# Transposing the quantised rows in fp32, with the rounding constant taken off by ScalarE's copies

## What is computed

```python
x = x + xattn(_layernorm(x), ctx, ctx, Wq, Wk, Wv, Wo, bo, mask)      # 16 heads of 64, causal, softmax
x = x + ffn(_layernorm(x), w_gate, w_up, w_down)

def _act_quant(x):
    scale = 127.0 / jnp.clip(jnp.max(jnp.abs(x), axis=-1, keepdims=True), 1e-05)
    return jnp.clip(jnp.round(x * scale), -128.0, 127.0) / scale
def _bitlinear(x, w):
    return jnp.einsum('bsi,oi->bso', _act_quant(x), _weight_quant(w))
def ffn(x, w_gate, w_up, w_down):
    return _bitlinear(jax.nn.silu(_bitlinear(x, w_gate)) * _bitlinear(x, w_up), w_down)
```

## Time and profile before

| | |
|---|---|
| timed runs | 828.57, 829.24, 829.48 us; median 829.24 |
| the profiled execution | span 827.9 us from its first to its last instruction |
| instructions in it | 17931 |
| mean granted clock of TensorE | 0.991 of full speed |
| HBM read and written | 15.64 MB and 4.19 MB, 24 GB/s over the span |

### The profile page before, as it was taken

How to read it: one execution, slowest core, us unless ns; L and a number is a source line. 1 busy time by engine, 2 the same in 40 slices (tenths; PEclk the granted TensorE clock), 3 DMA queues, 4 the chain that set the end, 5 groups by cost and what they waited for, 6 DMA issues and landing times.

```text
span 827.9 us, 17931 instructions
## 1 busy us (share of the span) xinstructions
PE 781.9 (94%) x5487; PEld 539.4 (65%) x5550; DVE 738.6 (89%) x1909; ACT 679.7 (82%) x1202; POOL 407.3 (49%) x404
## 2 busy tenths in 40 slices
PE   7899999999999999999999999999999999999873
PEld 5657666766766666676666667567666666766552
DVE  6759999999989998999989999899989999988994
ACT  4689888888888888888888898888888888888772
POOL 1235555454544644545455554455554555545551
PEclk9999999999999999999999999999999999999996
DMA  7200010100101010010100101010010100000000
GB/s 214 62 1 1 15 39 15 39 1 15 39 14 38 13 35 4 13 38 13 38 4 21 28 13 38 14 38 0 13 39 13 38 13 13 2 13 14 1 14 13
DMA packets 37108, 20.49 MB, mean 25 GB/s; under 512 B 1460, under 2 KB 36534, under 8 KB 37046
## 3 DMA queue, kind: packets, MB, share of 16 engines
q1 hardware_dynamic: 37046, 19.84, 8.3%
HBM read 15.64 MB, written 4.19 MB: 24 GB/s over the span
## 4 chain that ended last, share of the span: by engine, by line
PE 52%; DVE 31%; issue 11%; ACT 3%; DVEq 1%; POOL 1%; DMA 0%; POOLq 0%; ACTq 0%
PE ps_a L501 9%; PE ps_s L432 7%; DVE row_sum L821 5%; DVE xq_b L839 3%; PE ps_s L403 3%; DVE amax L778 2%; DVE hid L775 2%; PE ps_s L323 2%; PE ps_a L460 2%; PE ps_b L460 2%; PE ps_kv L403 2%; PE ps_s L325 2%; PE ps_kv L323 2%; PE ps_s L404 2%; PE ps_s L324 2%
## 5 line engine op out<-in xcount | busy, mean ns | idle before, releaser
L875 POOL TENSOR_TENSOR prob<-prob,row_max 128x1024 f32<-128x1024 f32 x64 | 122.0, 1906 | 194.1 <-DVE row_max L748 194.1
L521 ACT ACTIVATE vp<-ps_s 64x512 f32<-64x512 f32 x256 | 151.4, 591 | 32.8 <-PE ps_s L405 28.5
L893 POOL TENSOR_TENSOR prob<-prob,row_rec 128x512 f32<-128x512 f32 x128 | 130.9, 1044 | 56.2 <-DVE row_rec L823 56.2
L521 ACT ACTIVATE vp<-ps_kv 64x512 f32<-64x512 f32 x256 | 151.6, 592 | 5.4
L885 POOL TENSOR_TENSOR hid_b<-hid_q,neg_round 128x512 bf16<-128x512 f32 x64 | 66.6, 1041 | 130.1 <-DVE hid_q L792 130.1
L432 PE MATMUL ps_s<-kp,xn_t 128*64 128x512 f32 x512 | 124.0, 605 | 2.9 <-ACT vp L521 1.9
L501 PE MATMUL ps_a<-vp,prob_t 128*64 128x128 f32 x2048 | 125.9, 276 | 0.8 <-DVE x L770 0.6
L501 PEld LDWEIGHTS ps_a<-vp,prob_t 128*64 128x64 f32 x2048 | 110.6, 137 | 24.0 <-issue 16.4
L852 POOL TENSOR_TENSOR rs<-ve,neg_half 128x1 f32<-128x1 f32 x128 | 70.4, 550 | 35.5 <-DVE ve L670 25.4
L745 DVE TENSOR_TENSOR prob<-ps_s,bias_sb 128x1024 f32<-128x1024 f32 x64 | 78.2, 1222 | 10.7 <-PE ps_s L432 9.9
L521 ACT ACTIVATE kp<-ps_s 128x512 f32<-128x512 f32 x130 | 77.8, 598 | 12.0 <-PE ps_s L291 8.2
(11 more groups left out here) (176 smaller groups left out, 1767.6 us busy)
## 6 DMA issues: line engine op xcount, KB each, us to landing
x_in<-in_x SPq DMA_DIRECT2D x16, 256.0 KB, 3.0
ctx_in<-in_ctx SPq DMA_DIRECT2D x16, 256.0 KB, 3.4
x_res<-in_x SPq DMA_DIRECT2D x16, 256.0 KB, 2.8
out<-x SPq DMA_DIRECT2D x15, 256.0 KB, 2.3
kp<-in_L_xattn_Wk SPq DMA_DIRECT2D x1, 512.0 KB, 4.5
kp<-in_L_xattn_Wq SPq DMA_DIRECT2D x1, 512.0 KB, 5.3
kp<-in_L_xattn_Wv SPq DMA_DIRECT2D x1, 512.0 KB, 6.2
kp<-in_L_xattn_Wo SPq DMA_DIRECT2D x1, 512.0 KB, 6.1
```

Of the source, the lines that this page charges most:

```text
L521: copy = lambda dst, src, **kw: nc.scalar.activation(dst, src, ACT.Copy, **kw)
L875: p.tensor_tensor(prob[c % 2][:], prob[c % 2][:], rows(row_max[c % 2]), ALU.subtract).then_inc(shifted, 1)
L893: p.tensor_tensor(prob[c % 2][:, heads, :], prob[c % 2][:, heads, :], rows(row_rec[c % 2])[:, heads, :], ALU.mult).then_inc(normed, 1)
```

## The change

The subtraction of ROUND moves behind the transposes. xq and hid_q stay as fp32 rows that still hold ROUND; PE transposes them with the fp32 identity id_sb that the other transposes use, into fp32 views of the same PSUM banks; ACT's two copies to bf16 get a bias of -ROUND. The tiles xq_b, hid_b, id_bf and neg_round and the instructions that made them are gone. The guard on xqt_ready moves from L839 ahead to the instruction that makes xq, and L792's guard is now ht_ready. A slot has one DVE and one POOL instruction less, and ln2_step counts nine steps for ten.

```diff
-        ps_h = ps_b[:, 0:F // 2].bitcast(BF16)
+        ps_h = ps_b
-        ps_x = ps_u[:, 0:D // 2].bitcast(BF16)
+        ps_x = ps_u[:, 0:P]
...
-        LN1_STEPS, LN2_STEPS, H_STEPS = 3, 10, 7
+        LN1_STEPS, LN2_STEPS, H_STEPS = 3, 9, 7
...
-                    nc.tensor.transpose(ps_x[:, 0:P], xq_b[:], id_bf[:]).then_inc(xqt_ready, 1)
+                    nc.tensor.transpose(ps_x, xq[:], id_sb[:]).then_inc(xqt_ready, 1)
...
-                    pe.wait_ge(hb_ready, s - 2)
+                    pe.wait_ge(hq_ready, s - 2)
                     for k in range(FB):
-                        t = nc.tensor.transpose(ps_h[:, k * P:(k + 1) * P], hid_b[:, k * P:(k + 1) * P], id_bf[:])
+                        t = nc.tensor.transpose(ps_h[:, k * P:(k + 1) * P], hid_q[:, k * P:(k + 1) * P], id_sb[:])
...
-                    copy(xq_t[:], ps_x[:, :]).then_inc(xqt_evac, 1)
+                    copy(xq_t[:], ps_x, bias=-ROUND).then_inc(xqt_evac, 1)
...
-                    copy(flat(hid_t[:, :, :]), ps_h[:, :]).then_inc(ht_evac, 1)
+                    copy(flat(hid_t[:, :, :]), ps_h[:, :], bias=-ROUND).then_inc(ht_evac, 1)
...
-            dve.wait_ge(id_in, 16)
-            v.tensor_copy(id_bf[:], id_sb[:]).then_inc(const_set, 1)
...
-                        dve.wait_ge(hb_ready, s - 2)
+                        dve.wait_ge(ht_ready, s - 2)
...
-                    v.tensor_scalar(xq[:], xn2[:], qs2[:], ROUND, ALU.mult, ALU.add).then_inc(ln2_step, 1)
-                    dve.wait_ge(ln2_step, n + 9)
                     if ffn:
                         dve.wait_ge(xqt_ready, s - 1)
-                    v.tensor_scalar(xq_b[:], xq[:], ROUND, None, ALU.subtract).then_inc(xq_ready, 1)
+                    v.tensor_scalar(xq[:], xn2[:], qs2[:], ROUND, ALU.mult, ALU.add).then_inc(xq_ready, 1)
...
-                if live(it, c, 2):
-
-                    pool.wait_ge(hq_ready, s - 1)
-                    if live(it, c, 3):
-                        pool.wait_ge(ht_ready, s - 2)
-                    p.tensor_tensor(hid_b[:], hid_q[:], neg_round[:].broadcast_to([P, F]), ALU.add).then_inc(hb_ready, 1)
```

More of the change, by code:

```diff
@@ L90, in build @@
         neg_half = sb("neg_half", [P, 1])
-        neg_round = sb("neg_round", [P, 1])
         bias_sb = sb("bias_sb", [P, PAIRS, S])
@@ L114, in build @@
         xq = sb("xq", [P, D])
-        xq_b = sb("xq_b", [P, D], BF16)
         xq_t = sb("xq_t", [P, P], BF16)
@@ L124, in build @@
         hid_q = sb("hid_q", [P, F])
-        hid_b = sb("hid_b", [P, F], BF16)
-        id_bf = sb("id_bf", [P, P], BF16)
         hid_t = sb("hid_t", [P, FB, P], BF16)
@@ L174, in build @@
             "ctlo_ready", "biased", "max_done", "sum_step", "ln1_step", "xn_ready"))
-        x1_done, ln2_step, xq_ready, h_step, hq_ready, hb_ready, x2_done = (sem(n) for n in (
-            "x1_done", "ln2_step", "xq_ready", "h_step", "hq_ready", "hb_ready", "x2_done"))
+        x1_done, ln2_step, xq_ready, h_step, hq_ready, x2_done = (sem(n) for n in (
+            "x1_done", "ln2_step", "xq_ready", "h_step", "hq_ready", "x2_done"))
         shifted, normed, rstd1_done, rstd2_done, xres_ready = (sem(n) for n in (
@@ L341, in _ @@
                     pe.wait_ge(absum_done, 3)
-                    pe.wait_ge(const_set, 4)
+                    pe.wait_ge(const_set, 2)
                     mm(ps_kv[:, 0:3], ones_sb[:], f_sum[:, 0:3], start=True, stop=True).then_inc(mean_ready, 1)
@@ L641, in _ @@
             v.memset(neg_half[:], -0.5).then_inc(const_set, 1)
-            v.memset(neg_round[:], -ROUND).then_inc(const_set, 1)
             banks = [ps_s[:, 0:BANK], ps_s[:, BANK:], ps_kv[:, 0:BANK], ps_kv[:, BANK:],
@@ L859, in residual @@
                                 ALU.add).then_inc(xres_ready, 1)
-            pool.wait_ge(const_set, 3)
+            pool.wait_ge(const_set, 2)
             for t in range(2 * GP):
```

## The result

The changed kernel takes **830.55 us** (median of 15 runs, 829.36 to 832.38), the kernel before in the same measurement 828.65 us (15 runs, 828.07 to 829.48). The ratio is **1.0023, 95% interval 1.0016 to 1.0031**: 1.3 to 2.6 us slower, on either side of the 1.7 us that the prediction took as the limit of what can be told apart. The prediction said 830.4 us.

The account below looks back on a forecast made before the run. PE was taken as the bound, DVE some 0.2 us behind. +5.7 us until slot 60, -3.4 in slots 60 to 63 and -0.9 in the drain gave +1.4; carried over, 829.24 + 1.2 = 830.4 us, range 826.3 to 833.5.

Parts of the forecast that it names:

- PE bounds the slots, a relief of DVE is worth only PE's waits: Ordinary slots: PE is the bound, DVE some 0.2 us behind; relieving DVE gains at most 1.14 us per eight slots.
- +0.27 us a slot on PE: Five fp32 transposes for bf16 on PE: 0.22 us more for hid's four, 0.05 for xq's, in each slot.
- ACT at nothing: ACT's copies xq_t and hid_t, reading fp32 and subtracting a constant: 0 us, bounds 0.1 a copy either way.
- The jumps: Five loop jumps: ct_lo 0.28 us earlier, L453 behind it 0.22 longer, -0.06 each over two slots; xq_b's 0.96 not given back.
- L679's wait "still near 1.8 us": Sign to look for at the loop's jump: DVE's L679 still waits near 1.8 us, and starts earlier.
- Rival 3: The loop's jump gives back all of xq_b: 3.4 us less, 827.0 us; chance 0.08.
- Slots 61 to 64, -3.4 us: DVE-bound slots near the end: four steps give back 0.85 us each, -3.4 us with slot 60's own 0.27 included.
- The drain, -0.9 us: Pipeline drain from 806.83: clock may stay at 1.00, POOL's hid_b leaves the path; -0.9 us, 0 if the clock falls.
- Rival 1: POOL's hold-up moves from xq_b to xq, so nothing of DVE's time is saved: 837.7 us; chance 0.10.
- Rivals 2: The fp32 weight load shows in PE's transposes, +0.16 us a slot 57 times: 839.5 us; chance 0.08.
- rival 4: The longer transposes are covered by ACT, so 14 slots don't pay 0.27 us: 826.6 us; chance 0.12.

Follow-up runs that it names:

- hidq_twice: The changed kernel with the DVE instruction that writes hid_q done twice in each slot; 839.29 us, ratio 1.0125.
- pool_wait: The kernel before, still bf16, with POOL starting its second normalisation half only when DVE has written xq_b; 818.20 us, ratio 0.9868.
- short_norm: The kernel before with each POOL normalisation half cut to 4 of 8 heads, leaving half the probabilities unnormalised; 819.53 us, ratio 0.9891.
- hid_only: The kernel before with only hid transposed in fp32 and POOL's hid_b gone, xq_b kept; 839.35 us, ratio 1.0120.
- xq_only: The kernel before with only xq transposed in fp32 and xq_b gone, hid kept on POOL's bf16 copy; 821.12 us, ratio 0.9913.
- swap: The changed kernel with h_scale computed ahead of xq on DVE, so xq starts later; 842.02 us, ratio 1.0162.
- one_norm: The changed kernel with POOL's two normalisation halves as one instruction; 838.06 us, ratio 1.0109.
- unrolled: The kernel before with POOL's wait for xq_b and its loop written out, so no engine jumps; 812.54 us, ratio 0.9794.

## Why the prediction was right, step by step

- **PE bounds the slots, a relief of DVE is worth only PE's waits: right.** In the changed kernel each slot until the 60th, but for the five behind a jump, is as long as PE's instructions. PE's waits for xq_b come off, nothing else of DVE's 58.6 us does. hidq_twice bounds how far this goes: 0.5 us more on DVE costs nothing in 46 slots, all of it at the jumps and behind slot 60, and 0.35 us in the six slots where xq misses the seam.
- **+0.27 us a slot on PE: the sum right, its parts not.** Against pool_wait and short_norm, which show PE's period without waits, it is +0.26, +0.23 and +0.27. The four hid transposes cost 0.22, as worked out (hid_only). xq's transpose, put at 0.05, costs 0.10: in the changed kernel 0.17 us lie between it and the next (414.77 to 414.94), with bf16 0.06. What was mis-sized is this term: the 0.11 us rhythm inside a run was used for a transpose that stands behind the score matmuls. Together the parts would give 0.32 us; some 0.05 come back later in the slot in the change as a whole, and in xq_only they don't, which made that run 3 us longer than expected. Why they come back is open, so that the sum came out at 0.27 is in part luck.
- **ACT at nothing: right.** hid_t 597 ns before and after, xq_t 278 and 277.
- **The jumps: right in size, wrong in one sign.** The distance from the scores to the bias addition at slots 16, 24, 32, 40 and 48 was 4.07, 3.76, 3.79, 3.94 and 3.73 us and is 3.56, 3.75, 3.62, 3.45 and 3.46: 0.29 less on average (0.01 to 0.51), the forecast said 0.28. From the branch in DVE's sequencer to the start of the first instruction behind it, L679 or L672, it is 2.89 to 3.23 us in the five places before the change and 2.87 to 3.16 after it; one of each is 327.87 - 324.96 = 2.91 and 330.32 - 327.16 = 3.16 (below). So what counts is when the sequencer reaches the branch, and not how long the DVE instructions issued ahead of it still run. The sign that the prediction named did not come, though: L679's wait "still near 1.8 us". DVE stands idle for 2.72 us on average (13.6 in five places) where it was 2.07 (10.3). That sign contradicted the prediction's own sum: when 0.96 us of work go and L679 starts only 0.28 earlier, the wait must grow by 0.68. Rival 3, which would have given all of xq_b's 0.96 us back, is out: no place gave more than 0.51, in pool_wait a shorter xq_b (0.74 us less) leaves the distance at 3.83 us on average for 3.86, and PE still waits 4.2 us for ct_lo, for 5.8 before.

```profile
327.16 0.06 DVEq L198
```

```profile
327.18 1.94 PE L428 MATMUL ps_s<-kp,xn_t 128*64 128x512 f32 x8
330.32 0.69 DVE L672 TENSOR_TENSOR ct_lo<-ps_b,ct_hi 128x512 fp32r<-128x512 f32 x1 [2.89 <-issue]
...
331.14 0.65 PE L449 MATMUL ps_b<-id_sb,hid_q 128*128 128x128 f32 x4 [1.02 <-DVE ct_lo L672]
```

- **Slots 61 to 64, -3.4 us: right**, 5.81 - 2.36 = 3.45. L441 follows the scores by 1.87 us (787.89 to 789.76) where it was 2.99.
- **The drain, -0.9 us: right as a sum, by another split.** The clock did fall, to 0.54 of full speed in 810 to 813, which the prediction held for the less likely; but it fell later, when L441 and L449 of slot 64 had gone by at full speed, and slot 64 took 9.69 us (809.38 to 819.07) for 9.99. The last run of transposes cost what was worked out, 1.12 us at half clock for 0.61, and POOL's copy is off the path:

```profile
809.38 0.30 PE L441 MATMUL ps_u<-id_sb,xq 128*128 128x128 f32 x1 [2.59 <-DVE xq L830]
809.52 0.60 PE L449 MATMUL ps_b<-id_sb,hid_q 128*128 128x128 f32 x4
...
824.59 1.12 PE L449 MATMUL ps_b<-id_sb,hid_q 128*128 128x128 f32 x4 [3.49 <-DVE hid_q L785]
```
```profile
810.00:813.00 3.00, 2.62 (x15) 1.98 (x13) 0.74 (x2) 2.31 (x4) 0.15 (x1) 0.54 0.00 0
```

- **Rival 1 was the nearest miss, and the prediction's reading of the rows was wrong.** The prediction read the earlier trace rows as L839 held up by POOL and L835 free of it. L835 is not free: in swap, one_norm and short_norm the same instruction is held. The ends of the DVE instruction and of POOL's instruction beside it, put side by side, give one rule for all kernels here:

| kernel | DVE instruction | starts after POOL's first, us | ends after the end of POOL's instruction it started in | duration |
|---|---|---|---|---|
| before | xq_b | 1.16 | 0.08 (second half) | 0.97 |
| changed | xq | 0.83 | 0.08 (first half) | 0.29 |
| swap | xq | 1.14 | 0.08 (second half) | 0.99 |
| one_norm | xq | 0.77 | 0.08 (the only one) | 1.21 |
| short_norm | xq | 0.83 | 0.08 (second, shorter half) | 0.43 |

In the changed kernel, as in the kernel before, xq starts 0.21 us before the first half ends. Its end fits the rule, but it takes no longer there than the 0.29 us it has in the drain with no POOL instruction beside it, so a hold-up, if there is one, is hidden in its own duration. The margin is small: started 0.28 us later (hidq_twice, 1.11 for 0.83) xq is held through the second half, and with 0.31 later in every slot, as in swap, the change costs 13 us against the kernel before. How much less than 0.28 would do was not measured. That the forecast held against this rival was therefore in part luck: xq_b's wait for xqt_ready moved ahead of xq, and xq still started 0.83 us behind POOL. The Trainium skill (SBUF — State Buffer, "Who interferes with whom") says that a tensor_scalar can use the pair of ports that VectorE shares with GpSimd, that the engine which issues first then has the pair for its whole instruction, and that the other stands still altogether. The five rows of the table agree, and the prediction gave that rule too little weight against a row that it explains as well.
- **Rivals 2 and 4 are out**: the run of fp32 transposes lasts 0.60 us, and the slots with c = 4, where rival 4 had ACT cover the transposes, last 12.25 us for 12.02.
- **The closeness of 830.4 to 830.55 is luck in part.** The forecast added 1.2 us to 829.24, the median of three runs; the change measured 1.9 us, and it stands on 828.65. Two misses of 0.6 to 0.7 us cancel. The spans of the two profiled executions differ by 2.7 us. Of these, 1.4 lie between the first slot and the last instruction of the compute engines, which is what was forecast; 0.2 arose in the setup, and 1.1 behind that last instruction: 3.1 us to the end of the span, where it is 2.0 in the traces of the nine other kernels. The profiled execution was the slowest of the 15 (832.38 us). No run here looked at that last stretch.

## What to carry to other kernels

When one instruction takes three times as long as its neighbour with the same shape, look for what the other engine runs beside it before you rewrite the instruction: here one wait in the right place gained 10.8 us, and the rewriting of data types lost 1.9. Price a change half by half: here a gain of 8 us, from the wait that PE no longer had, was used up by a loss of 10 us, from longer work on PE, the engine that bounds. And where an instruction seems to pass unhurt beside another engine's, find out how much later it could start before that ends.

## What the runs showed of the hardware that had not been expected

- A DVE tensor_scalar of 128x128 that starts while a POOL tensor_tensor of 0.61 to 1.90 us runs ends no sooner than 0.08 us after that POOL instruction (five kernels in the table above, and short_norm's 15 places beside a third POOL instruction of 1.28 us). DVE's instructions with one column beside it are not held (in the changed kernel h_scale 0.26 us and clip 0.15), nor is the reduction amax (0.28 to 0.29).
- A 128x128 fp32 transpose behind the score matmuls keeps PE for 0.16 us until its next instruction, in a run each takes 0.11; with bf16 it is 0.06 and 0.055.
- At a jump of the loop 2.9 to 3.2 us lie between the branch in DVE's sequencer and the start of the first DVE instruction behind it, in all nine kernels that have the loop and whatever DVE still runs meanwhile. DVE is idle for 1.7 to 3.0 us of it. In straight code (unrolled) no such pause is left.
- One delay of 0.2 us appears at a fixed place of the loop in hidq_twice and in none of the other kernels; its cause is open.
